# Sorting tokens by expert and re-ordering a two-layer transformer kernel on one core

## The reference, cut to what matters

```python
x = x + attn_A(xn) + ffn_0(xn)          # ffn_0: x1 = xn + attn_B(xn); x1 + moe(x1)
x = x + attn_1(xn) + ffn_1(xn)          # xn: layernorm of the new x

def _moe(x, ln_w, ln_b, router_w, expert_wv, expert_proj):
    h = _layernorm(x, ln_w, ln_b)
    expert_idx = jnp.argmax(h @ router_w, axis=-1)
    for e in range(4):
        gate_raw, value = jnp.split(h @ expert_wv[e], 2, axis=-1)      # 128 -> 2 * 512
        y = gate_raw * sigmoid(gate_raw) * value @ expert_proj[e]       # 512 -> 128
        out = out + jnp.where((expert_idx == e)[..., None], y, 0.0)
```

## Time and profile before

| | us |
|---|---|
| median of 3 runs | 3768.03 |
| lowest, highest | 3767.74, 3790.23 |
| the profiled execution, its own time | 3783.69 |
| its span (first to last instruction) | 3781.9 |

### The profile page before, as it was taken

One profiled execution on the slowest core, in us unless ns is written; L12 is line 12 of the kernel. 1 busy time (PEld: TensorE's weight loads), 2 busy tenths in 40 slices (PEclk: granted clock), 3 DMA queues, 4 the chain that ended last, 5 costly groups with the idle time before them and its releaser, 6 DMA issues.

```text
span 3781.9 us, 53946 instructions
## 1 busy us (share of the span) xinstructions
PE 3371.3 (89%) x20319; PEld 1861.5 (49%) x20319; DVE 2505.3 (66%) x5526; ACT 1754.6 (46%) x4156; POOL 380.2 (10%) x676
## 2 busy tenths in 40 slices
PE   2789899999989899999989999998999999998954
PEld 1245455554545555554545545454555545454532
DVE  4555667676776767776776777677676767756453
ACT  0244544545455454545445454545545454554411
POOL 0000100202020010202011020201002020200101
PEclk6799999999999999999999999999999999999965
DMA  4120202020110202020020202001020201100000
GB/s 100 18 29 8 28 2 37 1 37 1 17 22 1 37 2 37 2 30 8 8 31 1 37 1 37 1 11 28 2 37 1 37 1 16 20 1 4 1 3 3
DMA packets 78714, 65.87 MB, mean 17 GB/s; under 512 B 8626, under 2 KB 75124, under 8 KB 78452
## 3 DMA queue, kind: packets, MB, share of 16 engines
q1 hardware_dynamic: 78452, 62.41, 11.5%
HBM read 15.47 MB, written 4.19 MB: 5 GB/s over the span
## 4 chain that ended last, share of the span: by engine, by line
PE 72%; DVE 13%; POOL 6%; ACT 4%; issue 3%; SPq 1%; DMA 1%; POOLq 0%; DVEq 0%; ACTq 0%
PE ps L1376 8%; PE ps L1359 6%; PE ps L1387 6%; PE ps L1394 6%; PE ps L1415 5%; PE ps L1494 5%; PE ps L1479 4%; PE ps L1337 4%; PE ps L1558 4%; DVE nma L1020 3%; PE ps L1580 3%; PE ps L1403 3%; PE ps L1349 3%; PE ps L1460 2%; PE ps L1362 2%
## 5 line engine op out<-in xcount | busy, mean ns | idle before, releaser
L718 ACT ACTIVATE share_a<-ps,nma 128x128 f32<-128x128 f32 (+3 forms) x1024 | 530.2, 523 | 426.4 <-DVE nma L1020 422.4
L1020 DVE TENSOR_REDUCE nma<-ps 128x2 f32<-128x256 f32 (+3 forms) x512 | 420.8, 824 | 426.1 <-PE ps L1362 421.8
L760 ACT ACTIVATE share_z<-ps 128x512 f32<-128x512 f32 (+1 forms) x704 | 368.9, 558 | 419.9 <-PE ps L1481 418.4
L1084 DVE TENSOR_REDUCE nmx<-ps 128x1 f32<-128x384 f32 (+3 forms) x704 | 426.4, 634 | 198.8 <-PE ps L1462 196.1
L614 POOL TENSOR_TENSOR vn<-va,rla 128x512 f32<-128x512 f32 x128 | 133.5, 1043 | 2952.3 <-DVE rla L976 2952.3
L1376 PE MATMUL ps<-share_a,vn 128*64 128x512 f32 (+3 forms) x2048 | 324.0, 462 | 38.5 <-POOL vn L614 37.0
L1460 PE MATMUL ps<-kst,qst 96*128 96x128 bf16 (+3 forms) x1024 | 264.5, 311 | 56.1 <-DMA kst<-part 36.3
L729 ACT ACTIVATE share_g<-ps 128x512 f32<-128x512 f32 x256 | 152.9, 597 | 347.5 <-PE ps L1387 344.5
L1337 PE MATMUL ps<-xnTd,wkqT 128*128 128x512 f32 x512 | 255.2, 622 | 28.2 <-ACT share_a L718 28.2
L1387 PE MATMUL ps<-h2Td,wgv 128*128 128x512 f32 x512 | 268.0, 605 | 2.8 <-ACT share_a L718 2.8
L1394 PE MATMUL ps<-h2Td,wgv 128*128 128x512 f32 x512 | 269.1, 607 | 0.0
(11 more groups left out here) (220 smaller groups left out, 5592.1 us busy)
## 6 DMA issues: line engine op xcount, KB each, us to landing
qst<-part SPq DMA_DIRECT2D x144, 128.0 KB
kst<-part SPq DMA_DIRECT2D x144, 128.0 KB
xin<-in_L_attn_x SPq DMA_DIRECT2D x16, 256.0 KB, 12.6
xk<-xn SPq DMA_DIRECT2D x16, 256.0 KB, 18.5
xres<-in_L_attn_x SPq DMA_DIRECT2D x16, 256.0 KB, 9.9
out<-xn SPq DMA_DIRECT2D x16, 256.0 KB, 11.8
wgv<-in_L_ffn_expert_wv SPq DMA_DIRECT2D x1, 2048.0 KB
qst<-share_h SPq DMA_DIRECT2D x48, 16.0 KB, 2.2
```

The lines of the kernel that those rows point to most:

```text
L718: activation(pa[:, h % 4, OFF[t]:OFF[t] + P * (t + 1)], ps[:, b + k, 0:P * (t + 1)], ACT.Exp, bias=nma[:, h, t:t + 1], accum_out=la[:, h, ...
L760: activation(pt[:, n % 2, h % 4:h % 4 + k, 0:wd], src, ACT.Exp, scale=SCALE_B)\
L1020: v.tensor_reduce(nma[:, 2 * p:2 * p + 2, t], ps[:, b:b + 2, 0:P * (t + 1)], AX.X, ALU.max, negate=True).then_inc(amax, 1)
L1084: v.tensor_reduce(nmx[:, h:h + k, t], src, AX.X, ALU.max, negate=True).then_inc(bmax_ready, 1)
```

## The change

**The experts work on sorted tokens.** A step `rank` (8 small bf16 products on PE) counts for each token how many before it chose the same expert; `place` (10 small DVE instructions) turns this into a row number, with each expert's tokens starting at a multiple of 128. At most 7 tiles of 128 tokens are then in use (`SORTED = NT + EXPERTS - 1`), and each has one expert. `scatter`: POOL writes the tokens' rows with four indirect DMAs to a tensor in DRAM, and SP reads the 7 tiles back (`hs`, 448 KB). `sort`: PE transposes the 7 tiles, ACT copies them out, and PE loads the 7 experts' numbers into registers. For a tile j, `gate` and `value` are one product each with 512 columns, whose weights are picked by the register; DVE's two instructions stay; `turn` transposes the result (4 transposes, one ACT copy), `down` is 4 products of 128x128, and ACT copies them out. `store_y`: ACT issues one DMA of the 448 KB to DRAM, and `gather`: POOL brings each token's row back with four indirect DMAs. `acc` is gone; `take_over` adds the gathered rows (`yg`) to `xacc`, and waits for them.

**Attention B's end and the router move** from the end of turn i-1 to the first half of turn i (stream `after`). The state that crosses the turn's edge is `ys`.

**Each engine has a list of its own** (`ORDERS`, with keys pe, dve, act and pool) in place of `ORDER`. SP's order: `keep_xn` and the load of `xres` first, then the load of the sorted tiles, the load of x, the shift rows, the stacks, the store.

**Layer 1's mixing in column groups.** `mix1` computes, in place of 128 output rows by 512 columns, two groups of 32 rows by 256 columns, side by side in the array; DVE keeps the own rows of 64 partitions by 256, and `project1` sums over 4 in place of 16.

**The feed-forward network uses two buffers** for `hf` and `sgf`, its step k = 3 and 4 of the rounding (three instructions) go from DVE to POOL, and so does `shift1`. Attention B's `project` writes PSUM bank 4 and not 7.

```diff
+SORTED = NT + EXPERTS - 1
-ORDER = [
-    ("take_over",), ("begin",), ("kq", 0), ("v", 0), ("kq", 1), ("ln2_stats",), ("scores", 0, 0), ("v", 1),
...
+ORDERS = dict(
+    pe=[
+        ("kq", 0), ("divide", 0), ("v", 0), ("divide", 1), ("kq", 1), ("scores", 0, 0), ("divide", 2),
...
+        3, 1), ("exps", 42), ("exps", 43), ("transpose_hq", 2), ("attend", 3, 2), ("transpose_hq", 3),
+        ("attend", 3, 3), ("down1",),
...
+                def load_sorted():
+                    sp.wait_ge(scattered, count(i, AHEAD["scattered"], 16 * NT))
+                    sp.dma_start(hs, h_sorted.rearrange("(t p) c -> p t c", p=P)).then_inc(hs_loaded, 16)
...
+                def scatter():
+                    pool.wait_ge(placed, count(i, AHEAD["placed"], 1))
...
+                    for t in range(NT):
+                        nc.gpsimd.indirect_dma_start(
+                            h_sorted, bass.IndirectOffsetOnAxis(place_i[:, t:t + 1].bitcast(U32), 0),
+                            xh[:, t, :], None).then_inc(scattered, 16)
+                def gather():
+                    pool.wait_ge(y_stored, count(i, DENSE["y_stored"], 16))
...
+                    for t in range(NT):
+                        nc.gpsimd.indirect_dma_start(
+                            yg[:, t, :], None, y_sorted,
+                            bass.IndirectOffsetOnAxis(place_i[:, t:t + 1].bitcast(U32), 0)).then_inc(y_gathered, 16)
+                def settle(n, a, e, r, m, dst):
+                    over = m.unsqueeze(2).to_broadcast([P, n, QBLOCK])
+                    link(nc.gpsimd.tensor_tensor(r, a, e, ALU.add))
+                    link(nc.gpsimd.tensor_tensor(r, r, e, ALU.subtract))
+                    return nc.gpsimd.tensor_tensor(dst, r, over, ALU.mult)
...
-                    link_b(v.tensor_copy(xp[:, :, :], xacc[:, :, :]))
+                    dve.wait_ge(y_gathered, count(prv, DENSE["y_gathered"], 16 * NT))
+                    link_b(v.tensor_tensor(xp[:, :, :], xacc[:, :, :], yg[:, :, :], ALU.add))
...
+                def sort():
+                    pe.wait_ge(placed, count(i, AHEAD["placed"], 1))
+                    pe.wait_ge(hs_loaded, count(i, DENSE["hs_loaded"], 16))
+                    pe.wait_ge(aexp_done, count(i, DENSE["aexp_done"], 4 * HEADS))
+                    for j in range(SORTED):
+                        ins = tr(ps[:, j // NT, tile(j % NT)], hs[:, j, :], idn)
+                    ins.then_inc(hs_psum, 1)
+                    for j in range(SORTED):
+                        expert[j] = pe.value_load(expert_i[0:1, j:j + 1], min_val=0, max_val=EXPERTS - 1)
...
-                    mm(ps[:, (2 * n) % 3, :], wgv[:, e, c * P:(c + 1) * P], h2Td[:, :],
+                    mm(ps[:, GATE_BANK[j % 2], :], hsT[:, tile(j)],
+                       wgv[:, bass.ds(expert[j], 1), 0:DFF].rearrange("c a f -> c (a f)"),
                        start=True, stop=True).then_inc(gate_psum, 1)
...
+                def down(j):
+                    pe.wait_ge(yT_ready, count(i, DENSE["yT_ready"], j + 1))
+                    for c in range(CHUNKS):
+                        ins = mm(ps[:, VALUE_BANK[j % 2], 0:C], ymT[:, j % 2, c, :],
+                                 wdn[:, bass.ds(expert[j], 1), c, :].rearrange("p a c -> p (a c)"),
+                                 start=(c == 0), stop=(c == CHUNKS - 1))
...
                 def mix1(half):
...
-                        ins = mm(ps[:, 7, :], v1[:, kt, :], pT[:, kt, :], start=(kt == 0), stop=(kt == NT - 1))
+                        for g in (2 * half, 2 * half + 1):
+                            ins = mm(ps[32 * g:32 * g + 32, 7, 0:T // 2], v1[:, kt, 32 * g:32 * g + 32],
+                                     pT[:, kt, T // 2 * (g % 2):T // 2 * (g % 2 + 1)],
+                                     start=(kt == 0), stop=(kt == NT - 1))
```

672 lines of the change are left out of this document (438 added, 234 removed), and 12 rows, old and new, of tables (ORDER, act).

## The result

Over four runs each, the kernel before took 3776.7 us (3767.7 to 3790.2) and the changed kernel 3600.5 us (3598.5 to 3605.0): a ratio of 0.953, 95% interval 0.950 to 0.957. That is 176 us less, where the forecast had 234 less. The profiled executions span 3781.9 and 3596.7 us, 185 us apart.

What follows compares the result with a forecast made beforehand. PE was taken to bound both halves of a turn. The terms summed to -13.7 us a turn, -219 us over 16 turns, and with filling and emptying -234, giving 3535 us on the median; range 3350 to 3700 us.

Steps and rivals of the forecast that it cites:

- price added work there at nothing: DVE in the first half: busy time going from 75 to about 85 of 114 us was to cost nothing; all exposed, +10.
- the half-rate stretch: PE after the gap of the register loads may come back at half rate: +1.7 us a turn, bounds 0 and 3.4.

## What to carry to other kernels

Where an engine with short operations in order feeds the one that bounds, its busy share says nothing of its slack. Ask at each tile what stands ahead of it on that engine, and do not price added work there at nothing: here it cost 0.4 to 1.0 of itself, in part as clock, which busy time hides. In most turns here a new wait of 1.5 to 2.5 us on TensorE cost once more what the half-rate stretch behind it took. When several releases fall within a microsecond, removing one shows the next: measure from the last common row. And before a transfer is moved, look at what else is issued at its new place: behind one rounding more the same gather took 11 us in place of 3.

## What the hardware showed beside that

DVE operations grew longer beside POOL's. The same addition of a bias (two inputs in SBUF) took 681 ns before and 1348 ns now that a `norm` runs on POOL at its side; a 128x56 difference went from 209 to 678 ns beside `shift1`, and an operation on 128x4 from 170 to 439 ns on average: two in three still take 170, the third, beside the rounding, 1.16 us. Groups of DVE, before and then after:

```profile
L1204 DVE TENSOR_TENSOR xp<-xp,b1bc 128x512 f32<-128x512 f32 x16 | 10.9, 681 | 0.0
L1174 DVE TENSOR_TENSOR dm<-rm 128x56 f32<-128x56 f32 x16 | 3.3, 209 | 0.0
L848 DVE TENSOR_SCALAR mv<-mv 128x4 f32<-128x4 f32 x48 | 8.2, 170 | 1.7
```

```profile
L1426 DVE TENSOR_TENSOR xp<-xp,b1bc 128x512 f32<-128x512 f32 x16 | 21.6, 1348 | 0.0
L1396 DVE TENSOR_TENSOR dm<-rm 128x56 f32<-128x56 f32 x16 | 10.8, 678 | 0.0
L1036 DVE TENSOR_SCALAR mv<-mv 128x4 f32<-128x4 f32 x48 | 21.1, 439 | 1.7
```

Over such rows DVE lost some 3 us a turn beside POOL's operations. By "SBUF — State Buffer" of the Trainium skill (Who interferes with whom), a DVE instruction with two SBUF inputs, or in a two-port mode, shares a port pair with GpSimd, and the later one stands still until the other is done; the first two rows agree. For the third, one input of 4 columns, no run here shows which mode it is in.

The work moved to POOL is slower there: 1901 ns for the 128x1024 subtraction against 1224 on DVE, a factor of 1.55.
